# Cross attention and routed FFN on one core: V projected one piece a step, zero products in the first steps, transposed maxima between the halves of up

## The reference

```python
# x: (16, 256, 128); ctx: (16, 64, 128); 16 heads of 8; 8 experts, 128 -> 512 -> 128
def xattn(q_in, ctx):                     # q_in = layernorm(x)
    Q, K, V = q_in @ Wq.T + bq, ctx @ Wk.T + bk, ctx @ Wv.T + bv
    w = softmax(Q_heads @ K_heads.T / sqrt(8))
    return (w @ V_heads).merged @ Wo.T + bo
def ffn(h):                               # h = layernorm(x)
    e = argmax(h.mean(tokens) @ Wr + br)  # one expert for each of the 16 sequences
    return relu(h @ W1[e] + b1[e]) @ W2[e] + b2[e]
x = x + xattn(layernorm(x), ctx)
x = x + ffn(layernorm(x))
```

## Time and profile before

| what | value |
|---|---|
| time, median of 3 runs | 174.6 us (174.48, 174.6, 176.12) |
| the profiled execution's own time | 176.33 us |
| its span, first to last instruction | 174.5 us |
| busy: PE, DVE, ACT, POOL | 150.8, 121.2, 111.3, 108.4 us |
| mean granted TensorE clock over the span | 0.922 of full |

### The profile page before, as it was taken

The page is one execution under the profiler, slowest core; times in us unless marked ns, Lnnn a source line. Parts: engine busy times, 40 slices in busy tenths (PEclk is TensorE's granted clock), DMA queues, the critical chain, the costliest instruction groups (busy, mean ns, idle before and its releaser), DMA issues.

```text
span 174.5 us, 4088 instructions
## 1 busy us (share of the span) xinstructions
PE 150.8 (86%) x1208; PEld 110.7 (63%) x1208; DVE 121.2 (69%) x334; ACT 111.3 (64%) x278; POOL 108.4 (62%) x186
## 2 busy tenths in 40 slices
PE   7875288689657999999999999899999989888793
PEld 5542153456443777787877778687877767567583
DVE  5489635858656889898898989787796937273200
ACT  3233774836485979797977969596775748244340
POOL 7276594065647299979887786655647484775310
PEclk9999755555996999999999999999999999999999
DMA  5647426372224273656546363745555452454250
GB/s 173 180 149 240 154 68 238 125 232 83 86 98 136 74 238 97 236 143 212 192 162 201 121 201 126 258 136 192 185 177 191 152 171 68 160 196 123 79 166 32
DMA packets 24582, 27.27 MB, mean 156 GB/s; under 512 B 4464, under 2 KB 19952, under 8 KB 24560
## 3 DMA queue, kind: packets, MB, share of 16 engines
q1 hardware_dynamic: 22704, 26.13, 45.9%
q10 hardware_dynamic: 1856, 0.88, 1.9%
HBM read 12.58 MB, written 2.10 MB: 84 GB/s over the span
## 4 chain that ended last, share of the span: by engine, by line
PE 67%; ACT 11%; DVE 6%; POOL 6%; issue 5%; DMA 2%; SPq 0%; ACTq 0%; POOLq 0%; DVEq 0%
PE bank_g L806 15%; PE bank_g L694 11%; PE bank_c L778 6%; PE bank_g L744 5%; PE bank_q L757 5%; PE bank_e L731 5%; PE bank_d L778 4%; PE bank_a L675 4%; ACT probs_t L522 3%; POOL xn L402 3%; PE bank_a L731 2%; DMA ctx_sb<-in_ctx_t 2%; PE bank_f L822 2%; PE bank_e L792 2%; ACT hid_t L562 2%
## 5 line engine op out<-in xcount | busy, mean ns | idle before, releaser
L806 PE MATMUL bank_g<-ew,hid_t 128*128 128x128 f32 x256 | 32.4, 280 | 1.9 <-ACT hid_t L562 1.7
L806 PEld LDWEIGHTS bank_g<-ew,hid_t 128*128 128x128 f32 x256 | 29.8, 191 | 6.4 <-issue 6.4
L994 DVE RECIPROCAL inv_sum<-denom 128x256 f32<-128x256 f32 x16 | 27.7, 1730 | 0.1
L402 POOL TENSOR_SCALAR xn<-x,mv,rstd 128x128 f32<-128x128 f32 x32 | 25.3, 798 | 1.7
L915 DVE TENSOR_TENSOR y_sb<-bank_g,x_b 128x256 f32<-128x256 f32 x16 | 6.8, 425 | 20.3 <-PE bank_g L806 19.8
L393 POOL TENSOR_TENSOR ve<-mv,eps_sb 128x2 f32<-128x2 f32 x16 | 3.1, 197 | 28.2 <-DVE mv L964 28.2
L530 ACT COPY heads_sb<-bank_g 128x512 f32<-128x512 f32 x16 | 9.4, 586 | 17.5 <-PE bank_g L694 17.5
L694 PE MATMUL bank_g<-probs_t,v_all 128*32 128x256 f32 x256 | 19.7, 432 | 0.4 <-DVE y_sb L915 0.3
L439 POOL TENSOR_TENSOR x_b<-x,ew 128x256 f32<-128x256 f32 x16 | 11.7, 728 | 11.7 <-DMA ew<-in_experts 11.0
L562 ACT ACTIVATE hid_t<-bank_c,ew 128x256 f32<-128x256 f32 x32 | 13.5, 473 | 7.9 <-PE bank_c L778 7.9
L778 PE MATMUL bank_c<-xn_t,ew 128*128 128x256 f32 x64 | 16.7, 383 | 0.0
(11 more groups left out here) (94 smaller groups left out, 404.3 us busy)
## 6 DMA issues: line engine op xcount, KB each, us to landing
q_stack<-q_parts SPq DMA_DIRECT2D x48, 128.0 KB, 2.3
ew<-in_experts SPq DMA_DIRECT2D x16, 320.0 KB, 3.0
ew<-in_experts SPq DMA_DIRECT2D x16, 258.0 KB, 2.7
denom<-heads_sb SPq DMA_DIRECT2D x16, 128.0 KB, 2.1
numer<-heads_sb SPq DMA_DIRECT2D x16, 128.0 KB, 2.1
out_y<-y_sb SPq DMA_DIRECT2D x16, 128.0 KB, 2.0
x_sb<-in_x SPq DMA_DIRECT2D x2, 768.0 KB, 5.1
k_stack<-k_parts SPq DMA_DIRECT2D x6, 128.0 KB, 2.1
```

Source lines behind the costliest of these rows:

```text
L402: nc.gpsimd.tensor_scalar(xn2[:, par, q, :], x1[:, n % 3, q, :], mv2[:, par, q, 0:1], rstd2[:, par, q, :], ALU.subtract, ALU.mult).then_in ...
L806: mm = nc.tensor.matmul(bank_g[:, 0, q * P:(q + 1) * P], hid_t[:, c, q * P:(q + 1) * P], w2_of(par, c), start=(c == 0 and q == 0), stop=(c ...
L994: nc.vector.reciprocal(inv_sum[:], denom[:, n % 2]).then_inc(inv_done, 1)
```

## The change

Three edits. (1) V pieces 1, 2, 3 are projected and copied in steps 1, 2, 3, one each; the waits follow: piece 2 waits for copy_heads of sequence 0, piece 3 for copy_heads of sequence 1 and add_x1 of sequence 0; the heads of sequences 1 and 2 wait for the copy of the piece that passed through bank_g just before. (2) Zero products: one and two in step 0, two in step 1, two in steps 2 and 3 (one between transpose1 and project_q, one after V), two in step 4. (3) In steps with an FFN, transpose_max and max_transposed move from before up and relu to between their halves.

```diff
-        VLATE = 4
-        FILLERS = {3: 2}
+        V_AT = {1: 1, 2: 2, 3: 3}
+        FILLERS = {1: 2, 2: 1, 3: 1, 4: 2}
...
             def v_of(c):
-                act.wait_ge(v_proj, max(c + 1, 4) if c >= 2 else c + 1)
+                act.wait_ge(v_proj, c + 1)
...
-                if t == 1:
-                    v_of(1)
-                if t == VLATE:
-                    v_of(2)
-                    v_of(3)
+                if t in V_AT:
+                    v_of(V_AT[t])
                 if live(t + 1) and t >= RAMP:
                     high_q(t + 1)
-                if live(t) and t >= RAMP:
-                    max_transposed(t)
                 if live(t - 5):
                     relu(t - 5, 0)
+                    if live(t):
+                        max_transposed(t)
                     relu(t - 5, 1)
...
-                if c == 2:
-                    pe.wait_ge(heads_out, VLATE - 1)
-                    pe.wait_ge(x1_done, VLATE - 2)
+                if c >= 2:
+                    pe.wait_ge(heads_out, c - 1)
+                if c == 3:
+                    pe.wait_ge(x1_done, 1)
...
-                if n == VLATE - 1:
-                    pe.wait_ge(v_act, 8)
+                if n in (1, 2):
+                    pe.wait_ge(v_act, 4 + 2 * n)
...
+                if t == 0:
+                    keep_busy(bank_e, 1)
                 if live(t + 1) and t < RAMP:
                     transpose1(t + 1)
+                    if 2 <= t < RAMP - 1:
+                        keep_busy(bank_f, 1)
                     project_q(t + 1)
...
                 if live(t - 1):
                     scores_t(t - 1)
+                if t == 0:
+                    keep_busy(bank_e, 2)
                 if live(t) and t < RAMP:
                     transpose_max(t)
...
-                if t == 1:
-                    project_v(1)
+                if t in V_AT:
+                    project_v(V_AT[t])
                 if live(t - 3) and t > 3:
                     project_o(t - 3)
-                if t == VLATE:
-                    project_v(2)
-                    project_v(3)
                 if t in FILLERS:
                     keep_busy(bank_c, FILLERS[t])
...
-                if live(t) and t >= RAMP:
-                    transpose_max(t)
                 if live(t - 5):
                     up(t - 5, 0)
+                    if live(t):
+                        transpose_max(t)
                     up(t - 5, 1)
```

## The result

The changed kernel takes 170.47 us (median of 4 runs, 169.32 to 170.90) against 175.36 (4 runs, 174.48 to 176.17): ratio 0.971, interval 0.963 to 0.979, faster. The forecast said 167.7, in a range of 164.8 to 171.5: the direction and the range held, the gain came out at 4.9 us of the 7 to 8 that I had reckoned.

What follows compares the result with a forecast made beforehand. PE's own stream was taken to bound the full steps, engine waits and a halved clock the ramp. 176.33 - 5.6 (ramp) - 2.4 (full steps) = 168.3, with a third of the median offset 167.7 us; range 164.8 to 171.5.

Steps and rivals of the forecast that it cites:

- the products of step 1: Two zero products after V piece 1: clock back at about 26.5 us, scores of step 2 1.2 us later.
- step 0's products: Zero products in step 0, in PE's waits for DVE: cost 0, without that cover 1.4 us.
- Steps 2 and 3: Ramp steps at full clock with V pieces 2 and 3: predicted gains 1.9 and 2.4 us, scores(4) at 39.8.
- Transpose1(6): Step 4, without the late V work and its waits: transpose1(6) 5.2 us earlier, at 48.1.
- so I expect no dip: Step 4's PE hole shrinks from 2.50 to about 1.3 us, so no clock dip; step 5's heads gain 0.87.
- my chain over POOL: Step 5: sequence 2's add_x1, norm2 and add_b2 on POOL come next, moving by -5.6 us or so.
- of the rivals the second: Clock rises later or falls again in steps 2 to 4, one to two steps lost: 170 to 171 us; chance 0.15.
- the first rival: Full steps gain nothing, ACT or DVE giving the 0.2 us back at down(1): 170.1 us; chance 0.13.
- the full steps: Steps 5 to 13: down no longer waits for relu(0), 0.2 us a step, 1.8 us in all.
- PE's own order: Full steps: once relu(0) starts earlier, PE's instruction order is the next limit, a step near 7.64 us.
- steps 14 and 15: Last full steps, no transpose1 between, wait for relu shows: gain 0.3 us each, 0.6 in all.
- My correction for the median: Median of runs is 1.7 us below the profiled execution; a third carried over, 168.3 to 167.7.

Runs made afterwards that it cites:

- The run with four more products: The changed kernel plus two zero products before transpose1(6) in step 4 and two before transpose2(1) in step 5: 168.53 us, ratio to before 0.962.
- edit 1 alone: Against the kernel before, only V pieces moved to one a step; zero products and transposed maxima as before: 172.79 us, ratio 0.989.
- The run with the memset: The changed kernel plus one useless 128x256 memset on DVE before the residual in steps 5 to 15: 171.28 us, one run.
- the run that was to take route_best out of it: The changed kernel with route_best after the second statistics on DVE and the maxima's DMA before the expert load on SP: 178.63 us, ratio to before 1.012.
- the profile of edit 3: Against the kernel before, only transposed maxima moved between the FFN halves: 174.19 us, median of 10, ratio 0.981.

## Why the prediction was right, and where its terms were off

The mechanism of the ramp held, step by step. Fall at 20, as said; the products of step 1 bring the clock back (predicted 26.5, measured 27); scores(2) later (+1.2 predicted, 27.32 - 25.63 = +1.7 measured). Of the excess, 0.23 stood already at scores(0), which came at 10.90 against 10.67, and step 0's products cost some 0.13, not 0 (the step went from 5.66 to 5.79). Steps 2 and 3 gave 2.1 and 2.4, predicted 1.9 and 2.4: scores(4) at 40.12, predicted 39.8. Transpose1(6) came 5.0 earlier, predicted 5.2.

The step that failed is "so I expect no dip", and with it step 5. It was to add 0.4 to the lead (5.2 to 5.6) and took 0.9 from it (9.58 to 10.49). I had written the hole of step 4 down to 1.3 (it was 1.12) and left out that transpose2(1) would wait too; my chain over POOL began with sequence 2. The norm2 of sequence 1 hangs on the residual of step 4, which lies ahead of the V work that was taken out. So its xn on POOL, here before and then in the changed kernel, came only 2.7 us earlier, and scores(5) 5.0:

```profile
51.35 1.58 POOL L402 TENSOR_SCALAR xn<-x,mv,rstd 128x128 f32<-128x128 f32 x2
```

```profile
48.61 1.58 POOL L402 TENSOR_SCALAR xn<-x,mv,rstd 128x128 f32<-128x128 f32 x2
```

Before, xn ended at 52.93, ahead of scores(5) at 53.68; now it ends at 50.19, behind scores(5) at 48.66, and PE stops for it. The run with four more products prices the dip at 1.36 us: without it scores(6) would have come 4.1 + 1.4 = 5.5 earlier (59.15 against 63.26 is 4.1), what the forecast said. So of the rivals the second, the clock that falls once more, came true, with its time of 170 to 171. The place was step 5, not steps 2 to 4. Of the first rival half came true, as the full steps gave half of their 0.2. The measured 170.47 lies outside the 165.5 to 169.2 to which I had given 0.56; it lies in the range because that was drawn to take in both rivals.

I credited the clock's return to the products alone. In one of four runs of edit 1 alone it returned early without them, at 33.4 us. For the sum this did no harm, since with the products it is back by 27. Two small readings of mine were off, with hardly an effect on the sum: between 21.22 and 37.53 PE stopped a fourth time, 0.46 us before 29.38, and 37.4 + 2.28 is 39.7, not 39.8.

The full steps: the wait of down for relu(0) is gone, as forecast. PE with the weight load of transpose2 (PEld), POOL and ACT in step 8 of the changed kernel, to set against the earlier trace rows, then two more rows of step 13 before:

```profile
79.99 0.38 PE L790 MATMUL bank_e<-cst,xn 128*128 128x128 f32 x2
80.21 2.03 PE L804 MATMUL bank_g<-ew,hid_t 128*128 128x128 f32 x16
...
82.09 0.20 PEld L820 LDWEIGHTS bank_f<-cst,xn 128*128 128x128 f32 x2
82.10 0.44 PE L820 MATMUL bank_f<-cst,xn 128*128 128x128 f32 x2
...
82.46 0.38 PE L673 MATMUL bank_a<-k_all,q_parts 32*128 32x256 f32 x1
```

```profile
80.46 1.58 POOL L402 TENSOR_SCALAR xn<-x,mv,rstd 128x128 f32<-128x128 f32 x2
```

```profile
79.19 0.84 ACT L562 ACTIVATE hid_t<-bank_c,ew 128x256 f32<-128x256 f32 x2
79.92 0.34 ACT L546 CAST negmax_t<-bank_f 16x256 fp32r<-16x256 f32 x1
```

```profile
126.42 0.38 PE L822 MATMUL bank_f<-cst,xn 128*128 128x128 f32 x2
126.74 0.38 PE L675 MATMUL bank_a<-k_all,q_parts 32*128 32x256 f32 x1
```

down starts 0.22 after transpose1, before 0.41, so 0.19 was won at that place. The mis-sized term is 0.2 a step for the step as a whole: it is 0.10. What I put next, "PE's own order", is not next. POOL's xn ends at 82.04 and transpose2 starts at 82.10, with its weights loaded only then. It starts 1.89 after down (before 1.85), and the next scores 0.36 after it (before 0.32), so some 0.09 of the 0.19 is lost again here. norm2 begins when DVE has reduced all maxima and added the residual, and those begin with the scores: a loop that PE can't shorten. The run with the memset confirms that the loop is there; that a step would fall to 7.64 without it is not shown, as the run that was to take route_best out of it made a longer wait. For steps 14 and 15 I forecast 0.3 each by the wait for relu; step 14 went from 7.83 to 7.75 as the others did, and in the tail this pair shows no gain (from the scores of step 15 to the end 39.93 before, 39.96 after).

The sum in the profiled executions: 4.1 up to scores(6) (4.47 from step 1 on, less 0.36 by which step 1 began later; predicted 5.6), from there to scores(15) 1.5 (71.3 to 69.8; predicted 2.4 with step 15), of which 0.6 is a stop of PE that the rows of before above don't show: one of 0.69 before scores_t in step 12 of before, with no releaser in the profile. The changed kernel has one of 0.57 in step 15, which takes it back from the tail. Without a stop as long there, five other kernels with edit 3 take 39.5 to 39.7 from the scores of step 15 to the end, and the four without edit 3 39.9 to 40.2: so step 15 is worth some 0.4, near the 0.3 of the forecast. 176.33 - 170.73 = 5.6. My correction for the median carried a further 0.6, which the longer series of before (175.3, 175.1, 174.9) doesn't support.

The sentence from the Trainium skill ("TensorE: Matmul & The Clock Gate", A second HAM failure mode: psum-queue depth-cycling), that short pauses between groups can bring the clock down, agrees with the changed kernel and with the run of four more products: the dip followed two pauses of about 1.1 us, and went with them. In the profiled execution with eight products in step 1 the same two pauses stood and the clock stayed, so such pauses do not always bring it down.

## What to carry to other kernels

Where two edits mend the same thing, here a pause of PE that keeps its clock low, time each alone before their gains are added: 3.6 and 4.0 us made 4.2 to 4.5 in the profiled executions. Look at the mean clock of every run, too, before one profile is taken for the kernel: the 3.6 came from an execution that three others by their clock did not repeat. Fill the holes in a ramp, the first above all: eight products in waits that stayed took another 3.4 us off steps 1 to 5 (42.46 to 39.10), and 3.3 off the median. And when a wait is taken out of a pipelined step, look for the loop around all engines, from one step's start to the next; the tenth that was missing here stood on POOL, whose last xn ends 0.06 us before the transpose that needs it.

## What was not expected

The clock's dip is not settled by the length of the pauses alone: in the profiled executions 1.12 and 1.07 us brought it down in the changed kernel and left it full where step 1 had its eight products. By the mean clocks each of these kernels goes either way (0.98 in one of four runs of the changed kernel, 0.99 in two of four with the eight products). What decides it in an execution isn't shown.

Why step 0 takes 5.7 us in some executions and 6.65 in others is half answered by the rows. The four records of zero products behind the first K projection take 1.91 us in the four profiles with late first scores, and 1.03 in the eight with early ones; here before and the run of four more products:

```profile
6.60 1.91 PE L622 MATMUL bank_f<-zeros 128*128 128x256 f32 x4
```

```profile
5.94 1.03 PE L619 MATMUL bank_f<-zeros 128*128 128x256 f32 x4
```

PE is then 1.8 us ahead at scores(0) (8.91 against 10.67), but DVE, for which V piece 0 waits 0.49 us in both, only 0.8 (V at 13.89 against 14.66), and step 0 grows by the difference. The clock reads 1.00 there in both, so why the records differ stays open.

Step 0's products may do more than they cost. In the profile of edit 3, which has none and starts early (9.05), the clock fell at about 12.2, in step 0; in the nine profiles with them it did not fall before 17.6. What they are worth by themselves was not tried.
